# State-space block on one core: seven instead of five states summed through transposes on TensorE in the last two scan orders

## The reference, cut to what matters

```python
xz = einsum('bchw,oc->bohw', x, in_proj_w)      # "in-projection": xx and z, 384 channels each
xx = gelu(depthwise_conv3x3(xx) + conv_b)
# for each order k, along l = 0 .. 2303:
delta = softplus(dts + dt_b)
h[d, n] = h[d, n] * exp(delta[d] * A[d, n]) + delta[d] * u[d] * B[n]
y[d]   += h[d, n] * C[n]                          # summed over n
# y = sum of the four orders + u * D; layer norm; * gelu(z); out projection
```

## Time and profile before

| | us |
|---|---|
| median of 3 runs | 14804.19 (14801.22 to 14804.39) |
| the profiled execution, its own time | 14815.26 |
| its span, first to last instruction | 14813.5 |
| one step of the scan (of 192), by `delta_u` in the third order | 54.72 |
| PE, DVE, ACT, POOL busy in the span | 12998.2, 13080.8, 10929.0, 10570.7 |

### The profile page before, as it was taken

One profiled execution on the slowest core, in us unless ns is written; L12 is line 12 of the kernel. 1 busy time (PEld: TensorE's weight loads), 2 busy tenths in 40 slices (PEclk: granted clock), 3 DMA queues, 4 the chain that ended last, 5 costly groups with the idle time before them and its releaser, 6 DMA issues.

```text
span 14813.5 us, 237782 instructions
## 1 busy us (share of the span) xinstructions
PE 12998.2 (88%) x61224; PEld 7809.4 (53%) x61224; DVE 13080.8 (88%) x13929; ACT 10929.0 (74%) x22434; POOL 10570.7 (71%) x4222
## 2 busy tenths in 40 slices
PE   6888988889888898888988889888898888988889
PEld 4555455554555545555455554555545555455554
DVE  8999689996899968999689996899969999599995
ACT  5888578875788757887578876788667886678865
POOL 6999069980799807998079970899709996099960
PEclk9999999999999999999999999999999999999999
DMA  3333023330334303343033430334203442043420
GB/s 113 129 129 122 25 94 128 130 119 21 100 129 132 109 21 105 129 138 99 21 111 127 138 95 21 117 131 136 86 21 124 129 136 82 21 131 128 137 75 26
DMA packets 907956, 1468.10 MB, mean 99 GB/s; under 512 B 38912, under 2 KB 891904, under 8 KB 893664
## 3 DMA queue, kind: packets, MB, share of 16 engines
q1 hardware_dynamic: 906560, 1452.37, 30.7%
HBM read 1350.07 MB, written 102.17 MB: 98 GB/s over the span
## 4 chain that ended last, share of the span: by engine, by line
issue 26%; PE 23%; POOL 22%; DVE 18%; DMA 5%; ACT 4%; DVEq 1%; POOLq 0%; SPq 0%; ACTq 0%
POOL area L1733 16%; DVE area L1173 12%; POOL area L1743 5%; PE ps L975 5%; PE ps L987 5%; DMA area<-bc_rows 5%; PE ps L710 4%; DVE area L1201 3%; PE ps L837 2%; ACT ps L1497 2%; PE ps L801 1%; ACT ps L1458 1%; POOL area L1718 1%; DVE area L365 1%; DVE area L1328 1%
## 5 line engine op out<-in xcount | busy, mean ns | idle before, releaser
L1173 DVE TENSOR_TENSOR_SCAN area<-ps,hst,area 128x384 f32<-128x384 f32 x9216 | 8576.7, 993 | 155.9 <-POOL area L1733 85.6
L1733 POOL TENSOR_TENSOR area<-area 128x1152 f32<-128x1152 f32 x3072 | 8008.9, 2644 | 63.7 <-POOL area L1718 35.9
L1497 ACT ACTIVATE ps<-area,a_neg 128x384 f32<-128x384 f32 x9216 | 5283.4, 579 | 1121.3 <-DVE area L1173 1076.7
L710 PE MATMUL ps<-area,ident 128*128 128x384 f32 x12624 | 4585.6, 500 | 866.1 <-POOL area L1743 816.2
L710 PEld LDWEIGHTS ps<-area,ident 128*128 128x128 f32 x12624 | 2268.8, 193 | 2576.7 <-POOL area L1743 991.8
L697 PE MATMUL ps<-ident,area 128*128 128x128 f32 x17280 | 2421.8, 277 | 4.5 <-ACT area L1466 4.5
L1653 ACT ACTIVATE area<-ps,t_neg,area 128x768 f32<-128x768 f32 x1728 | 1619.0, 987 | 1007.8 <-PE ps L975 1007.8
L1713 POOL TENSOR_TENSOR area<-area,ones 128x2304 f32<-128x2304 f32 x16 | 85.2, 5345 | 3102.1 <-ACT area L1427 2981.2
L697 PEld LDWEIGHTS ps<-ident,area 128*128 128x128 f32 x17280 | 2192.8, 193 | 56.9 <-ACT area L1466 9.7
L1466 ACT ACTIVATE area<-ps,area 128x384 f32<-128x384 f32 x2880 | 1639.6, 569 | 594.7 <-PE ps L688 592.0
L1743 POOL TENSOR_TENSOR area<-area 128x1152 f32<-128x1152 f32 x768 | 2028.6, 2641 | 33.8 <-ACT hst L1442 31.9
(11 more groups left out here) (163 smaller groups left out, 9403.2 us busy)
## 6 DMA issues: line engine op xcount, KB each, us to landing
area<-bc_rows SPq DMA_DIRECT2D x1536, 768.0 KB, 6.7
xz<-x_normed SPq DMA_DIRECT2D x144, 288.0 KB, 6.3
area<-in_x SPq DMA_DIRECT2D x18, 1728.0 KB, 10.5
area<-x_padded SPq DMA_DIRECT2D x24, 1250.0 KB, 12.1
z_raw<-z_st SPq DMA_DIRECT2D x144, 192.0 KB, 6.3
area<-z_raw SPq DMA_DIRECT2D x8, 3456.0 KB, 15.2
x_padded<-x_st SPq DMA_DIRECT2D x120, 200.0 KB, 7.7
x_normed<-area SPq DMA_DIRECT2D x9, 1728.0 KB, 8.1
```

Source lines behind the costliest of these rows:

```text
L710: m = e.matmul(ps[:, 5 + j, 0:CH], ident[:], hb[:, i % NH, j], start=i == 0, stop=i == N - 1)
L1173: e.tensor_tensor_scan(rev(hb[:, i % NH, j], k), rev(ps[:, 2 + j, 0:CH], k), rev(dbu[:, i % NH, j], k), hst[:, i, j:j + 1], ALU.mult, ALU. ...
L1497: e.activation(ps[:, 2 + j, 0:CH], dlt[:, par, j], ACT.Exp, scale=a_neg[:, j, k, i:i + 1]).then_inc(da, 1)
L1733: e.tensor_tensor(dbu[:, i % NH], du[:, par], row_b[:, q % 2, i % ROWS:i % ROWS + 1].broadcast_to([128, J, CH]), ALU.mult).then_inc(dbus, 1)
```

## The change

The sets of states, and the counts of semaphores that hang on them, become a `Plan` per order. Orders 0 and 1 keep the old sets (`FIVE`), and their engines' instructions stay in the same order. Orders 2 and 3 get `SEVEN`: states 3 (POOL's before) and 12 (DVE's before) are turned too. Their tiles share slots: 4, 5, 6 and 13, 14, 15 have two each; the first goes where the one tile went, the second behind the sums of DVE's states. ACT makes the second copy after the third decay. In the third order, which has in-projections, the z half moves from slot 14 to slot 13 and waits for DVE's product of state 11; its `unit_out` moves to ACT's program of state 14. Tiles use `ht` in turn by their number (`at % 3`) and no more by their place in the state. Counts that were a multiple of the step's number are now a multiple of the image's number and a constant.

```diff
-POOL_N = (0, 3, 6, 9)
-TURN_N = (1, 4, 7, 10, 13)
-DVE_N = tuple(i for i in range(N) if i not in POOL_N + TURN_N)
-SUM_AT = {0: 3, 2: 4, 3: 6, 5: 7, 6: 9, 8: 10, 9: 12, 11: 13, 12: 14, 14: 16, 15: 17}
+class Plan:
+    def __init__(self, pool, turn, units):
+        self.pool, self.turn, self.units = pool, turn, units
+        self.dve = tuple(i for i in range(N) if i not in pool + turn)
+        self.tiles = [(n, t) for n in turn for t in range(3)]
+        self.tiles.sort(key=lambda x: (x[0] + 1 + x[1], x[0]))
+        self.slots = {m: [a for a, (n, t) in enumerate(self.tiles) if n + 1 + t == m] for m in range(N + 2)}
+        self.turned = {n: self.tiles.index((n, 2)) + 1 for n in turn}
+        self.sum_at = {n: n + 3 for n in pool} | {n: n + 2 for n in self.dve}
+        self.order = tuple(sorted(self.sum_at, key=self.sum_at.get))
+        self.unit_after = tuple(max(n for n in self.dve if n < m - 1) for m in units)
+        self.np, self.nd, self.nt, self.ns = len(pool), len(self.dve), len(self.tiles), len(self.order)
+FIVE = Plan((0, 3, 6, 9), (1, 4, 7, 10, 13), (10, 14))
+SEVEN = Plan((0, 6, 9), (1, 3, 4, 7, 10, 12, 13), (10, 13))
+PLANS = (FIVE, FIVE, SEVEN, SEVEN)
+def made_d(b, q, n):
+    return b * D_ALL + (1 + D_TO[q] + n)
...
-UNIT_AT = (10, 14)
...
@@ PE
-                def turned_sum(g, m):
-                    n, at, tt = turn_at(m)
-                    e.wait_ge(turn_cp, g * NT + (NT + at + 1))
+                def turned_sum(q, at):
+                    n, tt = plan(q).tiles[at]
+                    e.wait_ge(turn_cp, made_t(b, q, at + 1))
                     for j in range(J):
-                        i = e.matmul(ps[:, 5 + j, tt * 128:(tt + 1) * 128], ht[:, tt, j * 128:(j + 1) * 128], ident[:],
+                        i = e.matmul(ps[:, 5 + j, tt * 128:(tt + 1) * 128], ht[:, at % 3, j * 128:(j + 1) * 128], ident[:],
                                      start=False, stop=False)
-                def slot(g, m):
-                    for i in SUM_ORDER:
-                        if SUM_AT[i] == m and i in POOL_N:
-                            state_sum(g, i)
-                    if turn_at(m):
-                        turn(g, m)
-                    if turn_at(m - 1):
-                        turned_sum(g, m - 1)
-                    for i in SUM_ORDER:
-                        if SUM_AT[i] == m and i in DVE_N:
-                            state_sum(g, i)
-                def unit(k, h, gd, i):
-                    e.wait_ge(hcs, gd + (1 + DVE_N.index((8, 12)[i]) + 1))
+                def tile(q, at):
+                    turn(q, at)
+                    if at:
+                        turned_sum(q, at - 1)
+                def slot(q, m):
+                    p = plan(q)
+                    for i in p.order:
+                        if p.sum_at[i] == m and i in p.pool:
+                            state_sum(q, i)
+                    for at in p.slots[m][:1]:
+                        tile(q, at)
+                    if m == N + 1:
+                        turned_sum(q, p.nt - 1)
+                    for i in p.order:
+                        if p.sum_at[i] == m and i in p.dve:
+                            state_sum(q, i)
+                    for at in p.slots[m][1:]:
+                        tile(q, at)
+                def unit(k, h, q, i):
+                    e.wait_ge(hcs, made_d(b, q, plan(q).dve.index(plan(q).unit_after[i]) + 1))
...
@@ DVE, the wait for a free buffer before scan i
-                        if free in TURN_N:
-                            e.wait_ge(turn_mm, g * NT + ((NT, 0)[before] + 3 * TURN_N.index(free) + 3))
+                        p = plan(q - before)
+                        if free in p.turn:
+                            e.wait_ge(turn_mm, made_t(b, q, p.turned[free] - before * p.nt))
                         else:
-                            e.wait_ge(ysum, g * NS + ((NS, 0)[before] + SUM_ORDER.index(free) + 1))
+                            e.wait_ge(ysum, made_s(b, q, p.order.index(free) + 1 - before * p.ns))
...
@@ ACT, after decay j of state i
-                            if j == 1 and i < 2 and last:
-                                turned_product(g - 1, *last, N - 1 + i)
-                            elif j == 1 and turn_at(i - 1):
-                                turned_product(g, k, c, i - 1)
+                            if i < 2 and last:
+                                for at in plan(q - 1).slots[N - 1 + i][j - 1:j] if j else ():
+                                    turned_product(*last, at)
+                            elif i >= 2:
+                                for at in plan(q).slots[i - 1][j - 1:j] if j else ():
+                                    turned_product(k, c, at)
...
-                        if k < UK and i - 1 in UNIT_AT:
-                            unit_out(h, UNIT_AT.index(i - 1))
+                        if k < UK and i - 1 in plan(q).units:
+                            unit_out(h, plan(q).units.index(i - 1))
...
@@ POOL
-                        if i in POOL_N:
+                        if i in plan(k * NC + c).pool:
                             times_c(g, i)
```

More of the change, by code:

```diff
@@ L61, with plan, counts, vars_of @@
 CT_T = HT + JC
-POOL_N = (0, 3, 6, 9)
-TURN_N = (1, 4, 7, 10, 13)
-DVE_N = tuple(i for i in range(N) if i not in POOL_N + TURN_N)
-NP, ND, NT = len(POOL_N), len(DVE_N), 3 * len(TURN_N)
-SUM_AT = {0: 3, 2: 4, 3: 6, 5: 7, 6: 9, 8: 10, 9: 12, 11: 13, 12: 14, 14: 16, 15: 17}
-SUM_ORDER = tuple(sorted(SUM_AT, key=SUM_AT.get))
-NS = len(SUM_ORDER)
+class Plan:
[13 more added lines that the diff above has]
+PLANS = (FIVE, FIVE, SEVEN, SEVEN)
+assert 0 in PLANS[0].pool and all(p.order[0] == 0 and p.dve[:3] == (2, 5, 8) for p in PLANS)
+def plan(q):
+    return PLANS[q % (K * NC) // NC]
+def counts(name):
+    n = [vars_of(plan(q))[name] for q in range(K * NC)]
+    return sum(n), [sum(n[:q]) for q in range(K * NC)]
+def vars_of(p):
+    return {"np": p.np, "nd": p.nd, "nt": p.nt, "ns": p.ns}
+(P_ALL, P_TO), (D_ALL, D_TO), (T_ALL, T_TO), (S_ALL, S_TO) = (counts(n) for n in ("np", "nd", "nt", "ns"))
+LAST = PLANS[-1]
+def made_p(b, q, n):
+    return b * P_ALL + (LAST.np + P_TO[q] + n)
+def made_d(b, q, n):
+    return b * D_ALL + (1 + D_TO[q] + n)
+def copied_d(b, q, n):
+    return b * D_ALL + (LAST.nd + D_TO[q] + n)
+def made_t(b, q, n):
+    return b * T_ALL + (LAST.nt + T_TO[q] + n)
+def made_s(b, q, n):
+    return b * S_ALL + (LAST.ns + S_TO[q] + n)
 ADD_AT = {5: 0, 8: 1, 11: 2}
@@ L755, in body @@
                             e.wait_ge(ct_cp, b * GM + GM)
-                        slot(g, m)
+                        slot(q, m)
                         if m < 3 and m in LATE_X and not last:
@@ L767, in scan_phase @@
                 walk(e, body)
[L768 to L773, removed]
+                q = K * NC - 1
+                for at in plan(q).slots[N]:
+                    tile(q, at)
+                turned_sum(q, plan(q).nt - 1)
+                state_sum(q, N - 2)
+                e.wait_ge(hcs, made_d(b, q, plan(q).nd))
                 for j in range(J):
@@ L1393, in _, with softplus @@
             group_std(1, 0)
-            def softplus(g, par, k, op, j, bank=1, h=None):
+            def softplus(g, par, k, op, j, bank=1, h=None, c8=None):
                 x, y = dlt[:, par, j], du[:, par, j]
@@ L1442, in hold_state, with c_copy @@
                     e.activation(hst[:, i], src, ACT.Copy).then_inc(carry, 1)
-                def c_copy(g, i, nxt, h=None):
-                    if i not in DVE_N:
+                def c_copy(g, q0, i, nxt, h=None):
+                    if i not in plan(q0).dve:
                         return
@@ L1534, in scan_phase @@
                 g = e.snap(b * 24 + 23)
-                turned_product(g, K - 1, NC - 1, N - 1)
-                turned_product(g, K - 1, NC - 1, N)
+                for m in (N - 1, N):
+                    for at in plan(K * NC - 1).slots[m]:
+                        turned_product(K - 1, NC - 1, at)
                 e.wait_ge(scan, b * 1152 + (1152 + 3))
                 hold_state(K - 1, NC - 1, N - 1)
-                c_copy(g, N - 1, None)
+                c_copy(g, K * NC - 1, N - 1, None)
                 e.preload_act_table_set("gelu_and_others")
@@ L1692, in _ @@
             e.memset(hst[:], 0.0).then_inc(carry, 16)
-            for s, v in ((dbus, 8), (ysum, NS), (pv, 4), (hcp, NP)):
+            for s, v in ((dbus, 8), (ysum, LAST.ns), (pv, 4), (hcp, LAST.np)):
                 e.sem_inc(s, v)
```

101 lines of the change are left out of this document (50 added, 51 removed).

## The result

The changed kernel takes 14696.7 us (median of 4 runs, 14691.1 to 14700.4), the kernel before 14802.7 beside it: ratio 0.9928, 95% interval 0.9912 to 0.9943. Forecast were 14693 and a ratio of 0.9925. Of the 111 us forecast, 106 came; the interval leaves out 1.

A forecast was written before the change was run, and what follows sets the result against it. POOL was taken as the strict bound, DVE next. Gains of 33 us in the third order and 78 in the last, together 111, took 14804.2 to 14693; forecast range 14660 to 14750 (chance 0.45), wider range 14605 to 14800.

The forecast's parts named there:

- The bound: Before the change POOL sets the pace at 54.66 us a step; DVE is next at 53.78.
- DVE's floor of 52.53: DVE's work a step after the change, 53.78 - 1.25; caps the gain at 2.19 a step, 210 us.
- Stall before scan 15: Third order: z unit in slot 13 delays `turn` (12,0) and the decay of 15; 1.2 us a step.
- Stretch of slots 4 to 8: Both changed orders: second tiles in slots 4 to 6 wait on one bank; costs about 0.3 us a step.
- the walk: Instruction-by-instruction timing of slots 4 to 8; put scan 8's buffer free at 12.9 against 12.63 wanted.
- Third and last order: Paces of 54.03 and 53.09 us a step, gains of 33 and 78 us.
- Waits of PE for POOL: Sign: PE's waits for POOL's product at `state_sum` fall by a third.
- Rival B: PE and ACT hide all added tiles, DVE runs gapless at 52.53: 14594 us, chance 0.12.
- the skill's rule: Judge PE's headroom by weight loads, 56% in the third order; by it the added tiles cost nothing.
- C: Slots 4 to 8 cost 1 to 1.5 a step instead of 0.3, eating the gain: 14789 us, chance 0.15.
- D: ACT becomes the bound through the tiles' round trip, a step of 55.7: 14896 us, chance 0.15.
- E: The order in slot 13 does no harm, both orders at 53.1 a step: 14650 us, chance 0.13.

The follow-up runs named there:

- e1: Kernel before with state 3 alone turned as well in the last two orders, z left in slot 14: 14759.5 us, ratio 0.9969.
- e2: Kernel before with state 12 alone turned as well in the last two orders, z in slot 13: 14809.6 us, ratio 1.0003.
- e3: The change with the z unit back in slot 14 in the third order: 14676.4 us, ratio 0.9913 to the kernel before.
- e10: The change with PE's z unit in the third order's slot 13 behind the sum of state 11, ahead of tile (12,0): 14658.8 us, ratio 0.9899.
- e4: The change with PE turning tile (12,0) before the sum of state 11 in slot 13: 14807.3 us, ratio 1.0002 to the kernel before.
- e11: e10 with seven turned states in the second order too: 14653.4 us, ratio 0.9897 to the kernel before.
- e9: e4 plus, in the last order's slot 13, a wait for DVE's product of 11 and two matmuls outside the result: 14734.6 us, ratio 0.9952.

## Why the prediction was right

- **The bound.** POOL strictly, DVE next: shown by e1 and e2 together.
- **DVE's floor of 52.53.** Third order 54.04 - 1.10 - 0.29 = 52.65, last 53.25 - 0.34 - 0.29 = 52.62 (0.34 is the 0.27 with the overlap that it replaces). The term was 0.1 short; which of the small distances makes it is not shown.
- **Stall before scan 15.** Forecast 1.2, by `turn` (12,0) ended at 4.95 and the decay at 6.6 after scan 13; measured 4.96 and a stall of 1.10. e3 and e10, which put the unit elsewhere, lose the gap or most of it: the cause is shown. The difference of 0.1 is that copy-out and decay start 0.37 apart and not 0.5; part is rounding, as 6.6 - 5.46 is 1.14.
- **Stretch of slots 4 to 8.** Forecast 0.3, measured 0.29. The largest part, 0.18, stands where the walk had it: scan 8 behind the last `turn` of state 4, forecast to end at 12.9 and measured at 12.78. That the second tiles make that `turn` late is argued from the walk; no run moved them.
- **Third and last order.** Forecast 54.03 and 53.09 a step, measured 54.04 and 53.25. In the third the floor's error and the stall's cancel, so that agreement to 0.01 is luck; in the last the floor and the overlap at scan 3 add up to 0.16 a step, 8 us, which is the larger part of what the forecast lacked.
- **Waits of PE for POOL.** Said to fall by a third; they fell from 37.5 to 2.1. POOL without its backlog has its products ready before PE's slot: the one of state 6 ended at 2770.28, and PE's sum of it began at 2772.59. The forecast did not size this, and nothing in its sum hung on it.
- **Rival B, and the skill's rule.** The added tiles did not hide. PE's weight loads rose from 184.78 of 329 us (56%) to 210.51 (64%), far from full, and the order on PE still cost 1.1 a step. e10 gets most of it back with the same work, so PE had throughput to spare, and what cost the time was what stood at the head of its queue. The Trainium skill ("Perfetto Trace Analysis", Identifying the Most-Contended Engine) judges PE's headroom by MFU (the operations done as a share of the peak) and the share of LDWEIGHTS; for throughput these runs agree, and such waits are not in that share.
- **Rivals C, D and E** did not occur in the change. C's mechanism, a late tile and a fallen clock that eat the gain, is what e4 shows, in slot 13 and not in 4 to 8; there the whole gain is lost. E's times are nearly e10's: the order in slot 13 does little harm only once the unit stands behind the sum.
- **Slips without effect.** (53 - 47.1)/16 is 0.37 and not 0.35, and D's 92 us are 96 x 0.96.

The kernel that beats both is e10 (e11 can't be told from it): 14658.8, 1.0% under the kernel before.

## What to carry to other kernels

When two engines run at 99% in step, price the relief of each alone: the second is worth nothing before the first. When work goes to engines that have time in the mean, walk the slot in which it lands, instruction by instruction, with distances from start to start; in an in-order queue what waits at the head holds up all behind it, and moving one unit behind others that were ready gave back 38 us here. Test such a move in every stage that it touches: the same edit was right in one order and cost 2.5 us a step in another.

## What the runs showed of the hardware that had not been expected

A wait of 2.77 us on PE, in a stream that is otherwise dense, went with a stretch at the lower clock in 30 of 48 steps, and not in the other 18. In one of the 30, from the start of `turn` (12,0) to the end of the sum of 11 it took 4.65 (3070.34 to 3074.99, e4) and 3.16 without that wait (3060.95 to 3064.11, e9). The 1.49 between them is what DVE's gap grew by, from 0.82 to 2.31. Dummy matmuls that split the wait were worth 73 us of 14807, and with them no last order had a stretch at the lower clock. In the change itself the granted clock of both orders is 1.00, where it was 0.99 and 0.96; PE's waits for POOL are nearly gone and its share is higher, but no run tells which of these keeps the clock up.
